# Two attention layers of a four-part kernel: batches staged in another order on TensorE, VectorE and ScalarE, with the group loops written out

## The chip, the core and the metric

The kernel runs on one core of a Trainium2 chip. The metric is the device time of one execution in microseconds (us). A core has five engines with queues of their own: PE (TensorE, matrix products; PEld is its weight loads), DVE (VectorE), ACT (ScalarE), POOL (GpSimd) and SP (SyncE, which here only issues transfers). Each queue is worked in the order of the program; engines wait for one another on semaphores, counters that one engine raises and another waits on. PE writes only to PSUM, eight banks of 512 float32 columns for 128 partitions.

## The reference, cut to what matters

```python
x = x + xattn0(layernorm(x), ctx)     # layer 0 attention
x = x + moe(layernorm(x))             # 32 experts, 4 per token
x = x + xattn1(layernorm(x), ctx)     # layer 1 attention
x = x + ternary_ffn(layernorm(x))

def xattn(hidden_q, kv_c, ...):       # 8 batches, 100 queries, 722 keys, 16 heads
    q_big  = einsum('bshk,hkq->bshq', (hidden_q @ Wq.T), w_kc_q)   # layer 0 also rotates it (rope)
    q_r    = einsum('bshq,hqr->bhsr', q_big, W_qr)
    k_r    = einsum('bld,hdr->bhlr', kv_rope, W_kr)
    scores = einsum('bhsr,bhlr->bhsl', q_r, k_r)
    attn   = softmax(scores, axis=-1)
    ctx_c  = einsum('bhsl,bld->bhsd', attn, kv_rope)
    ctx    = einsum('bhsd,hkd->bshk', ctx_c, w_kc_kv).reshape(b, s, H * K)
    return ctx @ Wo.T
```

Everything is float32 in the attention. The change touches only the two attention parts.

## The kernel before, in words

A layer's 16 heads are worked in four groups of four heads (`hg`, 0 to 3 in layer 0, 4 to 7 in layer 1). A group has four stages on PE.

**Head.** The projected queries `qc` of the group are made. In layer 0, `q_heads` (L643) makes a head's queries, `q_big` (L658) expands them, DVE and POOL rotate them, `q_r` (L670) and `q_c0` (L686) bring them to key space. In layer 1 there is no rotation, so two heads' weights are first folded into one matrix: `fold_m` (L700), `fold_mt` (L706), `fold_a` (L715), `fold_at` (L724), six pieces in all, each copied from PSUM by ACT (`fold`, through `copy`, L910) before the next can start. `q_r1` (L734) and `q_c1` (L748) then apply it. A group has two folds, u = 0 and 1, one for each pair of heads.

**Batches.** Eight batches `b` follow, staggered over ten steps `st`. The products of a batch are:

- `scores` (L757): six tiles of 128 keys by 400 columns (4 heads by 100 queries), which go in turn through PSUM banks 0, 1 and 2. Tile n waits until ACT has copied tile n - 3 out of its bank (semaphore `a_se`). ACT copies each tile into the SBUF buffer `Sb`, of which there are three (L991).
- DVE takes the largest value over the tiles, `mx` (L1056). PE transposes it (L842; semaphores `a_mx`, `a_mt`), DVE reduces it to `nmx`, with its sign changed (L1048), and PE spreads that over the partitions (L859; `a_nm`, `a_mb`).
- DVE adds it to the whole of `Sb` (L1052; `a_sb`), ACT takes the exponential in place (L1000; `a_ex`), DVE sums (L1065; `a_sum`).
- `softmax_sum` (L777) sums over partitions, DVE takes the reciprocal `rz` (L1062), `values` (L771) multiplies the exponentials with the keys for two halves `dc`, and DVE scales the result into `qc` (L1072; `a_cxe`).

In a step before, PE issues three tiles of batch st, the transposes of batch st - 1's maxima, the other three tiles, the spread, then `softmax_sum` and both halves of `values` of batch st - 2. DVE has the add of batch st - 1 ahead of the maxima of batch st. ACT has, in each step, the six copies of batch st, and behind them the exponential of batch st - 1.

**Tail.** In the last two steps there are no scores. PE puts a piece of the next group between: both halves of its first `q_heads` in layer 0, its first `fold_m` in layer 1.

**Output.** `ctxl` (L875) and the product with `Wo` (L885, L888) in fourteen pieces through banks 2 to 5, which DVE adds to `X` or `tail` (L1086; `a_add`). PE waits for all fourteen adds at the group's end (L891). SP then loads the next group's `wb` (L547) and, in layer 1, `wk` (L549), and behind them the weights of the group's second pair of heads (L535, L532).

PE, ACT, DVE, SP and POOL each run the groups in a hardware loop (`Fori`), with layer 0's first group written out ahead of it. In layer 1, POOL loads and ACT works pieces of the last layer's weights beside all that (`absolute`, L942): three per batch, with two buffers, each of which is loaded again only after ACT is done with it.

## Time and profile before

| | us |
|---|---|
| median of 3 runs | 3896.39 |
| lowest and highest | 3893.25, 3897.36 |
| the profiled execution | 3893.81 |
| its span, first to last instruction | 3892.1 |
| PE busy in it | 3594.0 (92%) |
| DVE busy | 1881.8 (48%) |
| ACT busy | 827.8 (21%) |
| layer 0's attention, about | 22 to 1333 |
| layer 1's attention, about | 2279 to 3302 |

The rows below have, for a timeline, the start and the time taken in us, the engine, the line, the operation, what it writes and reads, how many were merged into the row, and in brackets the idle time of the engine just before it with what ended it. `issue` is an idle time for which the profile shows no releaser. A float32 product here stands as two matmul records. PE's clock is shown by the granted clock of a stretch, of which 1.00 is full speed (2.4 GHz).

### The profile page before, as it was taken

The page shows a single profiled execution, that of the slowest core. Times are in us where ns is not written, and L with a number is a line of the kernel's source. Part 1 is how long each engine was busy: PE and PEld are TensorE (multiplying, and loading weights), DVE is VectorE, ACT ScalarE, POOL GpSimd, SP SyncE. Part 2 cuts the span into 40 slices and gives each one's busy share as a digit, 9 for nine tenths or more (in the row PEclk, how much of TensorE's full clock was granted, in tenths as well). Part 3 has the DMA queues.
Part 4 walks back from the last instruction along what each step waited for, and adds up shares of the span by engine and source line. Part 5 has one row for each costly group of instructions (what it writes and reads, how often), then busy time and mean ns, then how long its engine had stood idle before and what let it go on. Part 6 is the DMA issues. An engine that isn't in the chain of part 4 may idle for free.

```text
span 3892.1 us, 39006 instructions
## 1 busy us (share of the span) xinstructions
PE 3594.0 (92%) x14156; PEld 1763.2 (45%) x14157; DVE 1881.8 (48%) x1684; ACT 827.8 (21%) x1370; POOL 864.1 (22%) x778
## 2 busy tenths in 40 slices
PE   7899999999999869999999879999999998899999
PEld 4454455445445423333333335445455454554554
DVE  7784475466458441111111137538266285662561
ACT  1220131032022111111111125234143241220110
POOL 5500400310220022212222201000000000891780
PEclk9999999999999979999999989999999999999999
DMA  5621121122112186898779745245143250330320
GB/s 188 224 95 45 61 92 49 59 79 81 46 50 100 42 325 206 288 373 311 255 270 333 272 186 182 78 143 175 71 167 112 95 165 15 131 130 17 129 98 34
DMA packets 90366, 561.50 MB, mean 144 GB/s; under 512 B 10760, under 2 KB 12936, under 8 KB 76320
## 3 DMA queue, kind: packets, MB, share of 16 engines
q1 hardware_dynamic: 56080, 450.05, 30.3%
q0 software_dynamic: 30880, 93.75, 8.9%
q10 hardware_dynamic: 3312, 16.37, 1.2%
q8 instruction: 69, 1.13, 0.1%
q14 instruction: 25, 0.20, 0.0%
HBM read 522.39 MB, written 41.40 MB: 145 GB/s over the span
## 4 chain that ended last, share of the span: by engine, by line
PE 69%; DMA 10%; DVE 9%; issue 5%; POOL 5%; ACT 1%; SPq 1%; POOLq 0%; DVEq 0%; ACTq 0%
PE PS L771 12%; PE PS L757 11%; PE PS L1518 9%; PE PS L885 9%; PE PS L1895 4%; PE PS L1542 4%; DMA bias<-in_b 4%; POOL gtq L1814 4%; PE PS L643 3%; PE PS L658 3%; DVE mx L1056 2%; DMA stg<-in_F 2%; PE PS L875 2%; PE PS L734 2%; PE PS L1868 2%
## 5 line engine op out<-in xcount | busy, mean ns | idle before, releaser
L757 PE MATMUL PS<-qc,kvT 128*128 128x400 f32 x1536 | 544.9, 506 | 8.9 <-DMA kvT<-kvT_d 3.5
L1518 PE MATMUL PS<-W,hT 128*64 128x512 f32 x2208 | 514.4, 609 | 33.3 <-DMA bias<-in_b 32.8
L771 PE MATMUL PS<-Sb,kvN 128*128 128x400 f32 (+1 forms) x1536 | 529.6, 501 | 2.5 <-DVE qc L1072 2.5
L771 PEld LDWEIGHTS PS<-Sb,kvN 128*128 128x128 f32 (+1 forms) x1536 | 293.4, 191 | 231.7 <-issue 11.2
L1116 POOL TENSOR_TENSOR qrope<-rt,rt 128x400 f32<-128x400 f32 x192 | 209.9, 1114 | 827.8 <-DVE rt L1027 827.8
L757 PEld LDWEIGHTS PS<-qc,kvT 128*128 128x128 f32 x1536 | 290.0, 193 | 223.1 <-issue 22.6
L1607 DVE TENSOR_TENSOR gu<-PS,bias 128x512 f32<-128x512 f32 x69 | 47.7, 691 | 679.3 <-PE PS L1518 679.3
L1868 PE MATMUL PS<-xh,wq 128*128 128x400 f16 x2048 | 354.2, 335 | 18.6 <-DVE wq L1744 17.7
L1814 POOL TENSOR_SCALAR gtq<-stg,thr 128x1024 f16<-128x1024 f32 x96 | 311.7, 3259 | 114.6 <-DMA stg<-in_F 114.6
L885 PE MATMUL PS<-wb,ctxl 128*128 128x512 f32 x768 | 331.7, 593 | 4.7 <-ACT ctxl L910 4.7
L1056 DVE TENSOR_REDUCE mx<-Sb 128x400 f32<-128x2400 f32 x64 | 274.3, 4285 | 106.6 <-ACT Sb L991 106.6
L1518 PEld LDWEIGHTS PS<-W,hT 128*64 128x64 f32 x2208 | 155.4, 140 | 331.7 <-issue 300.4
L1868 PEld LDWEIGHTS PS<-xh,wq 128*128 128x128 f16 x2048 | 199.3, 98 | 173.4 <-issue 21.6
L1065 DVE TENSOR_REDUCE sums<-Sb 128x400 f32<-128x2400 f32 x64 | 265.6, 4149 | 0.0
L1027 DVE TENSOR_TENSOR rt<-PS,ropeq 128x800 f32<-128x800 f32 x192 | 180.8, 984 | 164.0 <-PE PS L658 163.9
L1542 PE MATMUL PS<-W,actT 128*64 128x512 f32 x1104 | 250.3, 596 | 2.5 <-ACT actT L1647 2.5
L991 ACT ACTIVATE Sb<-PS 128x400 f32<-128x400 f32 x320 | 159.0, 502 | 414.6 <-PE PS L757 414.6
L1052 DVE TENSOR_TENSOR Sb<-Sb,PS 128x2400 f32<-128x2400 f32 x64 | 169.9, 2654 | 158.3 <-PE PS L859 158.3
L885 PEld LDWEIGHTS PS<-wb,ctxl 128*128 128x128 f32 x768 | 145.3, 190 | 189.7 <-issue 179.9
L1086 DVE TENSOR_TENSOR X<-PS,X 128x512 f32<-128x512 f32 x96 | 66.4, 692 | 305.3 <-PE PS L885 305.3
L1744 DVE SCALAR_TENSOR_TENSOR wq<-stg,nthr,gtq 128x1024 f16<-128x1024 f32 x64 | 141.7, 2253 | 112.2 <-POOL gtq L1814 112.2
L1000 ACT ACTIVATE Sb<-Sb 128x2400 f32<-128x2400 f32 x64 | 141.1, 2205 | 237.4 <-DVE Sb L1052 237.4
(272 smaller groups left out, 3625.9 us busy)
## 6 DMA issues: line engine op xcount, KB each, us to landing
W<-in_W SPq DMA_DIRECT2D x34, 4096.0 KB
W<-in_W SPq DMA_DIRECT2D x34, 2048.0 KB
kvT<-kvT_d SPq DMA_DIRECT2D x64, 768.0 KB, 5.8
kvN<-kvN_d SPq DMA_DIRECT2D x64, 768.0 KB, 4.3
stg<-in_F SPq DMA_DIRECT2D x32, 1536.0 KB, 6.3
absin<-in_F POOLq DMA_DIRECT2D x48, 512.0 KB, 4.2
hn<-in_F POOLq DMA_DIRECT2D x48, 512.0 KB, 3.8
wb<-in_WB SPq DMA_DIRECT2D x8, 2560.0 KB, 9.4
```

The source lines that it names most:

```text
L757: mm = nc.tensor.matmul(PS[:, lc % 3, 0:GW], kvT[b % 2][:, dc, lc * P:(lc + 1) * P], qc[:, dc, b, :], start=dc == 0, stop=dc == CC - 1)
L771: mm = nc.tensor.matmul(PS[:, 6 + dc, 0:GW], kvN[b % 3][0:k, lc, dc * P:(dc + 1) * P], Sb[b % 3][0:k, lc, :], start=lc == 0, stop=lc == LC ...
L885: mm = nc.tensor.matmul(PS[:, 2 + n % 4, :], ctxl[:, a, m * P:(m + 1) * P], wb[:, w:w + 512], start=a == 0, stop=a == HA - 1)
L1027: ins = nc.vector.tensor_tensor(rt[k % 2][j][:, :, :].rearrange("p i (b s) -> p i b s", b=BH), src, tab, ALU.mult)
L1052: nc.vector.tensor_tensor(sb, sb, PS[:, 4, 0:GW].unsqueeze(1).to_broadcast([P, LC, GW]), ALU.add).then_inc(sem(f"{p}_sb"), 1)
L1056: nc.vector.tensor_reduce(mx[:, :], Sb[st % 3][:, :, :].rearrange("p c n -> p n c"), AX, ALU.max).then_inc(sem(f"{p}_mx"), 1)
L1065: nc.vector.tensor_reduce(sums[:, :], Sb[(st - 1) % 3][:, :, :].rearrange("p c n -> p n c"), AX, ALU.add).then_inc(sem(f"{p}_sum"), 1)
L1116: ins = nc.gpsimd.tensor_tensor(qrope[k % 4][:, i, :], rt[k % 2][0][:, i, :], rt[k % 2][1][:, 1 - i, :], ALU.add)
L1518: mm = nc.tensor.matmul(PS[g * BS:(g + 1) * BS, 2 + u % 2, :], hT2[k][:, c, half * BS:(half + 1) * BS], W2[:, q, o:o + N1], start=c == 0, ...
L1542: mm = nc.tensor.matmul(PS[h * BS:(h + 1) * BS, 4 + u % 2, :], actT[:, j, g * BS:(g + 1) * BS], W2[:, u % NQ_W, o:o + DH], start=c == 0, s ...
L1814: nc.gpsimd.tensor_scalar(gtq[q][:, w, :], stg[q][:, w, :], thr[:, w:w + 1], None, ALU.is_gt).then_inc(sem("f_gt"), 1)
L1868: mm = nc.tensor.matmul(PS[:, 4 * q + 2 * w + half, 0:HALF], wq[q][:, w, c, :], xh[part][:, c, half * HALF:(half + 1) * HALF], start=c == ...
```

## The change

- On PE, the six tiles of a batch's scores are issued together; behind them come the transposes of the previous batch's maxima, `softmax_sum` and the first half of `values` of the batch before that, the spread, and the second half of `values`.
- On DVE, the maxima of batch st are ahead of the add of batch st - 1, and the scaling into `qc` is ahead of the sums.
- On PE, the next group's pieces are spread over the last two batches. In layer 1 this is now the whole fold of its first pair, with PSUM banks 0 and 1, and ACT's six copies of it move with it; the SBUF tiles that it writes get places that the batches don't use.
- The wait for all of a group's adds moves from the group's end to the first products that write those banks; in layer 0 `q_big` starts with banks 4 and 5.
- PE's and ACT's group loops are written out; DVE, POOL and SP keep theirs.

The core of the diff:

```diff
+        def big_bank(k):
+            return 4 - 2 * (k % 2)
+
+        def fold_bank(u, n):
+            return ((1, 0, 1, 0, 1, 0), (1, 3, 4, 5, 2, 3))[u][n]
...
                 if k >= 2:
                     pe.wait_ge(sem(f"{p}_rt"), NQ * hg + k - 1)
+                elif hg > 0:
+                    pe.wait_ge(sem(f"{p}_add"), 2 * MT * hg - 2 * (1 - k))
...
+                for st in range(B):
+                    pe.wait_ge(sem(f"{p}_kt{st % 2}"), 16 * (4 * hg + st // 2 + 1))
+                    scores(hg, st, range(LC))
+                    if st == 0:
+                        continue
                     if st == 1 and ly == 1:
                         q_c1(hg, 6)
+                    largest(st - 1)
                     if st == 1 and ly == 1:
                         q_c1(hg, 7)
...
                     if st >= 2:
                         softmax_sum(hg, st - 2)
+                        values(hg, st - 2, 0)
+                    spread(st - 1)
+                    if st >= 2:
+                        values(hg, st - 2, 1)
+                largest(B - 1)
+                if more and ly == 0:
+                    q_heads(hg + 1, 0, 0, range(KC))
+                elif more:
+                    fold_m(hg + 1, 0)
+                values(hg, B - 2, 0)
+                if more and ly == 1:
+                    fold_mt(hg + 1, 0)
+                spread(B - 1)
+                values(hg, B - 2, 1)
+                softmax_sum(hg, B - 2)
+                if more and ly == 0:
+                    q_heads(hg + 1, 0, 1, range(KC))
+                elif more:
+                    fold_a(hg + 1, 0)
+                values(hg, B - 1, 0)
+                if ly == 0:
+                    softmax_sum(hg, B - 1)
+                elif more:
+                    fold_at(hg + 1, 0)
+                values(hg, B - 1, 1)
+                if ly == 1:
+                    softmax_sum(hg, B - 1)
...
-                pe.wait_ge(sem(f"{p}_add"), 2 * MT * (hg + 1))
-            with pe.Fori(g0 + (ly == 0), g0 + HG) as hg:
-                body(hg)
+            if ly == 1:
+                fold_all(g0, 0)
+            for hg in range(g0, g0 + HG):
+                body(hg, first=hg == 0)
```

On ACT, in a step `st`, nothing moves between the copies and the exponential, except that in layer 1 the copies of `q_c1`'s last two pairs go behind the six copies of step 1.

PE at the start of a group's batches, layer 0's first group, before. `kvT` is the key tile of `scores`, `mx` marks the transposes of the maxima, `nmx` the spread, `sums` the `softmax_sum`, `kvN` the `values`:

```order
L757 MATMUL PS<-qc_94,kvT_172416_95 128x400 x12
L757 MATMUL PS<-qc_94,kvT_178560_96 128x400 x6
L842 MATMUL PS<-cst_50,mx_65 100x128 x4
L757 MATMUL PS<-qc_94,kvT_178560_96 128x400 x6
L859 MATMUL PS<-cst_50,nmx_68 128x100 x4
L757 MATMUL PS<-qc_94,kvT_172416_95 128x400 x6
L842 MATMUL PS<-cst_50,mx_65 100x128 x4
L757 MATMUL PS<-qc_94,kvT_172416_95 128x400 x6
L859 MATMUL PS<-cst_50,nmx_68 128x100 x4
L777 MATMUL PS<-sums_66,cst_50 128x400
L771 MATMUL PS<-Sb_111616_71,kvN_184704_97 128x400 x12
```

The same place with the change:

```order
L767 MATMUL PS<-qc_93,kvT_172416_94 128x400 x12
L767 MATMUL PS<-qc_93,kvT_178560_95 128x400 x12
L844 MATMUL PS<-cst_50,mx_65 100x128 x4
L850 MATMUL PS<-cst_50,nmx_68 128x100 x4
L767 MATMUL PS<-qc_93,kvT_172416_94 128x400 x12
L844 MATMUL PS<-cst_50,mx_65 100x128 x4
L787 MATMUL PS<-sums_66,cst_50 128x400
L781 MATMUL PS<-Sb_111616_71,kvN_184704_96 128x400 x6
L850 MATMUL PS<-cst_50,nmx_68 128x100 x4
L781 MATMUL PS<-Sb_111616_71,kvN_184704_96 128x400 x6
```

The six tiles (twelve products) of a batch are no longer parted, and the second transposes of maxima have moved from the middle of batch 2's scores to behind them.

DVE at the same place, before:

```order
L1056 TENSOR_REDUCE mx_65<-Sb_111616_71 128x400
L1048 TENSOR_REDUCE nmx_68<-PS 100x4
L1052 TENSOR_TENSOR Sb_111616_71<-Sb_111616_71,PS 128x2400
L1056 TENSOR_REDUCE mx_65<-Sb_121216_72 128x400
L1065 TENSOR_REDUCE sums_66<-Sb_111616_71 128x400
```

DVE there with the change:

```order
L1086 TENSOR_REDUCE mx_65<-Sb_111616_71 128x400
L1082 TENSOR_REDUCE nmx_68<-PS 100x4
L1086 TENSOR_REDUCE mx_65<-Sb_121216_72 128x400
L1091 TENSOR_TENSOR Sb_111616_71<-Sb_111616_71,PS 128x2400
L1105 TENSOR_REDUCE sums_66<-Sb_111616_71 128x400
```

Batch 1's maxima have moved ahead of batch 0's add.

ACT there with the change; `Sb<-PS` are the copies, L1030 the exponential. The order is that of before, where the lines are L991 and L1000:

```order
L1017 ACTIVATE Sb_121216_72<-PS 128x400 x5
L1017 ACTIVATE Sb_121216_72<-PS,cst_50 128x400
L1030 ACT_TABLE_LOAD
L1030 ACTIVATE Sb_111616_71<-Sb_111616_71 128x2400
L1017 ACTIVATE Sb_130816_73<-PS 128x400 x5
```

Nothing has moved: batch 0's exponential still stands between the copies of batch 1 and those of batch 2.

## Rows read from the trace of the kernel before

**Rows 1.** The page, part 1: busy us, share of the span, instructions.
```profile
PE 3594.0 (92%) x14156; PEld 1763.2 (45%) x14157; DVE 1881.8 (48%) x1684; ACT 827.8 (21%) x1370; POOL 864.1 (22%) x778
```
**Rows 2.** Stretch 842.6:913.1: us; busy PE, PEld, DVE, ACT, POOL; PEclk, DMA, GB/s.
```profile
842.60:913.10 70.50, 70.50 (x234) 40.81 (x233) 59.82 (x25) 21.26 (x28) 0.00 (x0) 1.00 0.24 90
```
**Rows 3.** Timeline of PE, start of the batches, second group of layer 0.
```profile
482.53 12.35 PE L757 MATMUL PS<-qc,kvT 128*128 128x400 f32 x36 [0.66 <-ACT qc L910]
...
507.73 1.09 PE L842 MATMUL PS<-cst,mx 128*100 128x128 f32 x4 [2.85 <-DVE mx L1056]
...
524.30 2.18 PE L757 MATMUL PS<-qc,kvT 128*128 128x400 f32 x6
```
**Rows 4.** Timeline of DVE and ACT there.
```profile
491.52 4.23 DVE L1056 TENSOR_REDUCE mx<-Sb 128x400 f32<-128x2400 f32 x1 [17.02 <-ACT Sb L991]
496.48 0.69 DVE L1048 TENSOR_REDUCE nmx<-PS 100x4 f32<-100x512 f32 x1 [0.74 <-PE PS L842]
500.86 2.65 DVE L1052 TENSOR_TENSOR Sb<-Sb,PS 128x2400 f32<-128x2400 f32 x1 [3.69 <-PE PS L859]
...
503.55 2.20 ACT L1000 ACTIVATE Sb<-Sb 128x2400 f32<-128x2400 f32 x1 [2.44 <-DVE Sb L1052]
505.66 1.27 ACT L991 ACTIVATE Sb<-PS 128x400 f32<-128x400 f32 x3
```
**Rows 5.** Timeline of PE, the same start in the third group.
```profile
803.49 12.35 PE L757 MATMUL PS<-qc,kvT 128*128 128x400 f32 x36 [0.66 <-ACT qc L910]
...
842.59 2.85 PE L757 MATMUL PS<-qc,kvT 128*128 128x400 f32 x8
```
**Rows 6.** Timeline, the same start in layer 1's second group.
```profile
2583.96 12.35 PE L757 MATMUL PS<-qc,kvT 128*128 128x400 f32 x36 [0.79 <-DVE qc L1043]
...
2599.26 1.06 ACT L942 ACTIVATE hn<-hn 128x1024 f32<-128x1024 f32 x1 [3.76 <-DMA hn<-in_F]
...
2624.68 1.51 PE L757 MATMUL PS<-qc,kvT 128*128 128x400 f32 x4
```
**Rows 7.** Timeline of PE where layer 0's second, third and fourth groups start.
```profile
384.49 1.61 PE L658 MATMUL PS<-qhk,wc_h 128*128 128x400 f32 x4 [1.61 <-DVE hn L1086]
385.94 2.18 PE L643 MATMUL PS<-xnT,wq_h 128*128 128x400 f32 x6
...
702.67 3.03 PE L658 MATMUL PS<-qhk,wc_h 128*128 128x400 f32 x4 [5.80 <-issue]
705.49 3.58 PE L643 MATMUL PS<-xnT,wq_h 128*128 128x400 f32 x6
...
1020.42 3.03 PE L658 MATMUL PS<-qhk,wc_h 128*128 128x400 f32 x4 [5.24 <-issue]
```
**Rows 8.** DMA queues, 384 to 697 us: PE's instruction fetch (packets, MB, share).
```profile
q8 instruction: 8, 0.13, 0.2%
```
**Rows 9.** DMA queues, 2584 to 3089 us: there is no q8 row.
```profile
q14 instruction: 2, 0.02, 0.0%
```
**Rows 10.** Timeline of PE, layer 1, end of the first group, start of the second.
```profile
2466.56 0.93 PE L859 MATMUL PS<-cst,nmx 100*128 100x100 f32 x4 [4.40 <-DVE nmx L1048]
...
2539.57 1.92 PE L888 MATMUL PS<-wb,ctxl 128*32 128x512 f32 x16
2543.29 0.32 PE L706 MATMUL PS<-cst,mT_sb 128*128 128x128 f32 x1 [1.80 <-DVE hn L1086]
2543.98 3.04 PE L715 MATMUL PS<-wq_h,m_sb 128*64 128x512 f32 x8 [0.37 <-ACT m_sb L910]
...
2561.08 1.53 PE L700 MATMUL PS<-wc_h 128*64 128x128 f32 x24
```
**Rows 11.** DMA, 2530 to 2575 us: KB each, us to landing; 2544 to 2557, all packets.
```profile
wb<-in_WB SPq DMA_DIRECT2D x1, 2560.0 KB, 9.0
...
DMA packets 850, 4.99 MB, mean 384 GB/s; under 512 B 92, under 2 KB 92, under 8 KB 727
```
**Rows 12.** Timeline of PE, layer 0's last group, the spread of batch 7.
```profile
1254.70 0.93 PE L859 MATMUL PS<-cst,nmx 100*128 100x100 f32 x4 [5.83 <-DVE nmx L1048]
```

More of the change, by code:

```diff
@@ L229, in build @@
         wk = pl1.put("wk", [P, HA // 2, DC])
+        mT_sb = pl1.put("mT_sb", [P, K])
+        m_sb = pl1.put("m_sb", [P, 2 * R])
         pa.at = max(pa_sb.at, pl0.at, pl1.at)
@@ L235, in build @@
         wb = pa.put("wb", [P, WB_N])
+        aT_sb = pa.put("aT_sb", [P, D])
         ropek = pprep.put("ropek", [P, 2, LC, DC])
@@ L777, in softmax_sum, with fold_all @@
                 nc.tensor.matmul(PS[:, 5, 0:GW], ones, sums[:, :], start=True, stop=True).then_inc(sem(f"{p}_z"), 1)
-            def next_group(hg, n):
-                if ly == 0:
-                    q_heads(hg, 0, n, range(KC))
-                elif n == 0:
-                    fold_m(hg, 0)
+            def fold_all(hg, u):
+                fold_m(hg, u)
+                fold_mt(hg, u)
+                fold_a(hg, u)
+                fold_at(hg, u)
             def body(hg, first=False):
@@ L814, in body @@
                 else:
-                    fold_mt(hg, 0)
-                    fold_a(hg, 0)
-                    fold_at(hg, 0)
                     q_r1(hg, 0)
@@ L849, in body @@
                         pe.wait_ge(sem(f"{p}_qce"), 16 * hg + 16)
-                    if st >= B:
-                        if first:
-                            next_group(hg + 1, st - B)
-                        else:
-                            with pe.If(hg < g0 + HG - 1):
-                                next_group(hg + 1, st - B)
-                    if 1 <= st <= B:
-                        pe.wait_ge(sem(f"{p}_nm"), B * hg + st)
-                        for a in range(HA):
-                            mm = nc.tensor.transpose(PS[:, 4, a * S:(a + 1) * S], nmx[0:S, a:a + 1].to_broadcast([S, P]), ident[0:S, 0:S])
-                        mm.then_inc(sem(f"{p}_mb"), 1)
                     if st >= 2:
                         softmax_sum(hg, st - 2)
-                        for dc in range(CC):
-                            values(hg, st - 2, dc)
+                        values(hg, st - 2, 0)
[25 more added lines that the diff above has]
+                    softmax_sum(hg, B - 1)
                 pe.wait_ge(sem(f"{p}_wb"), 16 * (hg + 1))
@@ L967, in body @@
                 else:
-                    for n in range(6):
-                        fold(hg, 0, n)
                     c_qr1(hg, 0)
@@ L983, in body @@
                         c_qc1(hg, n, 0)
+                more = hg < g0 + HG - 1
                 for st in range(B + 1):
@@ L992, in body @@
                                                  bias=bias).then_inc(sem(f"{p}_se"), 1)
-                            if st == 1 and ly == 1 and lc % 3 == 2:
-                                for j in range(2):
-                                    c_qc1(hg, 6 + lc // 3, j)
+                            if st == 1 and ly == 1 and lc == LC - 1:
+                                for n in range(6, 8):
+                                    for j in range(2):
+                                        c_qc1(hg, n, j)
                             if ly == 1 and lc in (1, 4):
                                 absolute(hg, 3 * st + lc // 3)
+                    if st == B and ly == 1 and more:
+                        for n in range(2):
+                            fold(hg + 1, 0, n)
                     if st >= 1:
@@ L1005, in body @@
                         eng.dma_start(acc_t[bass.ds(hg * ZROWS, ZROWS), :], A["zero"].to_broadcast([ZROWS, D])).then_inc(sem("m_fill"), 16)
+                if ly == 1 and more:
+                    for n in range(2, 6):
+                        fold(hg + 1, 0, n)
                 for n in range(2 * HA):
@@ L1008, in body @@
                     copy(ctxl[:, a, half * HALF:(half + 1) * HALF], PS[:, 3 + n % 2, 0:HALF], "lt", 8 * hg + n + 1, "lte")
-            if ly == 0:
-                body(0, first=True)
-            with eng.Fori(g0 + (ly == 0), g0 + HG) as hg:
-                body(hg)
+            if ly == 1:
+                for n in range(6):
+                    fold(g0, 0, n)
+            for hg in range(g0, g0 + HG):
+                body(hg, first=hg == 0)
         def att_vector(dve, ly):
```

76 lines of the change are left out of this document (36 added, 40 removed).

## The prediction, made before the changed kernel was run

> **What bounds the kernel now.** I read the page's busy times first: PE is busy for 92% of the span, 298 us are left over [rows 1], so an attention change can only win by closing PE's gaps. Then I read the windows over the middle of a group. Over four batches, 70.5 us or 17.6 us each, PE is busy for all of 70.5 us at full clock, DVE for 59.8 [rows 2]. There nothing waits, and the order of the products can't matter unless it makes a wait. So the question is what the change does at three places: the start of the batches, their end, and the passage to the next group. There the timeline of PE shows its gaps, and the timelines of DVE and ACT show what ends them.
>
> The start, from the first score tile to that of batch 3, holds 34.6 us of work on PE: three scores of 8.06, one `values` of 8.06, one `softmax_sum` of 0.7, and transposes. It takes 39.1 us in the undisturbed case [rows 5], 41.8 in the second group, where the clock was low after an idle 2.85 [rows 3], and 40.7 in layer 1 with 1.75 more work [rows 6]. The other five, read the same way, are 42.2 and 40.5 in layer 0, and 41.7, 40.5, 40.5 in layer 1.
>
> **The steady batches.** The same products, adds and reductions are issued. In the new order, counted from the start of batch st's scores, PE does: scores to 8.1, transposes of maxima to 8.5, `softmax_sum` and half of `values` to 13.2, spread to 13.6, other half to 17.6. DVE: nmx 8.7 to 9.4, maxima 4.23 long to 13.7, add 2.65 long to 16.4, reciprocal, scaling, sums to 24.2, that is 6.6 in the next batch; PE wants them at 8.5. ACT's exponential is over at 18.6, and the first copy of the next batch is due at 19.3. Every wait has slack: 0 us, with 17.6 per batch as before.
>
> **The start of the batches: a new wait.** This is the term against the change. DVE now does batch 1's maxima ahead of batch 0's add, ACT has the exponential of batch 0 ahead of the copies of batch 2, and at this point PE has no `values` to fill in. Layer 0, from the first score tile at 0, durations from [rows 4], offsets as there (maxima start 9.0 after the scores, nmx 0.67 after its transposes, the add 0.54 after the spread):
> - PE: scores 0 and 1 to 16.1, transposes to 16.6. nmx is 16.8 to 17.5, so PE idles 1.0 until the spread at 17.6. Scores 2 start at 18.0.
> - DVE: maxima of batch 1 from 17.5 to 21.7, add of batch 0 to 24.3. Before, that add began with the spread [rows 4].
> - ACT: exponential of batch 0 from 24.4 to 26.6. Only then comes the copy of batch 2's first tile, over at 27.1.
> - PE: three tiles fit into banks 0 to 2 by 22.0, the fourth waits for that copy: 5.2 us idle. Scores 2 end at 31.2, `softmax_sum`, `values`, two transposes end at 40.8.
>
> 40.8 against 39.1 is 1.7 us more. And the low clock comes on top: after idle times of 5.80 the next products took 3.03 and 3.58 us for 1.61 and 2.18, a loss of 2.8 [rows 7]; after 2.89 there was none [rows 5]. An idle 5.2 lies near the first, I take 2.2, bounds 0 and 2.8. So 43.0 per group, four make 172, and the first group keeps another 1.7 us of low clock from its wait for the keys. 173.7 against 163.6 before: **+10**, bounds +1 and +12.
>
> Layer 1 is worse, because ACT's pieces of `absolute` stand in its queue. The fourth waits for its data until 15.3 after the start, and is over at 16.5 [rows 6]; copies behind it are late. Before, PE had `q_c1` and transposes to do there. Now the sixth tile of batch 1 waits for the copy of its third: 2.1 idle. Then ACT copies tiles, a fifth piece (1.25), the last tile at 19.5, and `q_c1`'s pairs; PE idles 0.9 for them; spread 21.3, scores 2 from 21.7. Maxima 20.5 to 24.8, add to 27.4, exponential to 29.7, one more piece of `absolute` to 30.7, first copy over at 31.2; the fourth tile has waited since 25.7, 5.5 us. Scores 2 end at 35.2, batch 3 starts at 45.0. With 2.2 of low clock 47.2, four times 188.8, against 163.4: **+25**, bounds +8 (the data comes in time, no low clock) and +29.
>
> **Batches' end.** Layer 0 before loses 0.45 and some transposes' order; counted through in the new order, with the scaling ahead of the sums, PE never waits: 46.6 from the last scores to `ctxl` against 47.3, -0.7 for each of three passages, **-2**. Layer 1 before idles 4.40 at the spread of batch 7 [rows 10], with low clock behind it, 44.2 in all. Now `fold_mt`, `fold_a`, `fold_at`, 3.4 us, stand in its place; I count idles of 0.6, 0.35 and 1.9 and 43.6 us: -0.6 each. In the last group of a layer there is nothing to put between: idles of 2.1, 0.8 and 3.7 where one of 5.83 stood [rows 12]: 0, bounds -1 and +1 for both.
>
> **The passage, layer 0.** The first passage waits 1.61 for the adds [rows 7]; `q_big` in banks 4 and 5 needs twelve of the fourteen, which are there when PE is done: -1.6. The second and third are jumps back in the loop, and idle 5.80 and 5.24 with no releaser, then run 2.8 and 2.7 at low clock [rows 7]. Such a group has 8 fetches of instructions [rows 8]; the first group, written out, has its fetches and no such idle. Written out, these go: -8.6 and -7.9. What is late next is DVE, whose loop stays: its rotation could start up to some us later, but `q_big` needs it only from its third product on, 5.4 us in; 0, at most +1.5 each. Sum **-18**, bounds -18 and -15.
>
> The Trainium skill, page "Runtime: NRT & Kernel Launch", section "Instruction fetch mechanics", says that a taken branch whose target is outside a window of two pages forces a fetch, and that kernels therefore rather unroll. By it layer 1's three jumps would stall too, and writing them out would give some 12 us more. The trace doesn't bear that out: those three idle 1.80 at most, no more than their adds need [rows 10], and in 505 us there is not one fetch on q8 [rows 9].
>
> **The passage, layer 1.** Before, from the end of L888 at 2541.5, PE waits 1.80, folds with low clock, and reaches the second `fold_m` at 2561.08, 19.6 later [rows 10]. The folds are gone from here, so `q_r1` (10.9) starts at once and `fold_m` could come 12 us in. But it reads weights that SP asks for only behind `wb` and `wk`, after the last add: `wb` lands 9.0 after 2542.93, and 1.97 MB behind it at the 384 GB/s of this stretch need 5.1 [rows 11]: 2557.0, 15.5 after PE's end. So 4.1 are won, and an idle 3.2 in front of `fold_m` may bring low clock, 1.8: 2.3, bounds 1 and 7.9. With the batches' end: -2.9 each, three make **-9**, bounds -5 and -25.
>
> The Trainium skill, "DMA: Bandwidth & Descriptors", section "Where 436 GB/s comes from", has 436 GB/s as the ceiling; by it the 5.1 would be 4.5, and the sum 2 us less.
>
> **Sum.** +10 +25 -2 -18 -9 = +6 us. The profiled execution was 3893.8, its span 3892.1 and 1.7 around it; it lay 2.6 under the median of 3896.4. 3893.8 + 6 = 3900; against the median 3902. I predict 3901.
>
> **Rivals.**
> 1. *The start costs little.* The low clock doesn't come after the new idle, and `absolute`'s data is there. For it: one of four groups in layer 0 and three of four in layer 1 had none after 2.9 idle; against: after the attention's idles of 3.5, 4.4, 5.2 and 5.8 the clock was low each time. Then the starts cost +1 and +8, the passages stay: +9 -29 = -20, 3876. With only half of that, 3890, it would just count as no change. 18%.
> 2. *The start costs more* (the slower side, beyond my own forecast). ACT's queue in layer 1 is a chain: if a transfer for `absolute` lands later, the first copy of batch 2 is later by the same, and PE's idle grows one for one. It decides from about 1 us more per group, or when low clock comes twice in one start, after 2.1 and after 5.5: 2.8 more. +3 in each of eight groups is +24: 3920 or so with the rest. 20%.
> 3. *Steady batches get a wait*, because DVE's chain runs 1.9 us ahead of PE's need, no more. Each 0.2 us per batch would be 64 x 0.2 = 13: 3914. Against: 59.8 of 70.5 busy [rows 2]. 7%.
> 4. *Writing out does not remove the idle* at layer 0's jumps, because it is something else than the jump: +16.5, 3917. For it: `issue` names no releaser. Against: the first passage, without a jump back, has none. 7%.
>
> My forecast has 48%. Its own range is 3893 to 3909. What a measurement can tell from no change is 0.2%, 7.8 us, so from 3888.6 to 3904.2. The forecast's part below 3904 is same, about 30 of 48, the rest slower; rivals 2 to 4 are slower; rival 1 is faster but for its nearest end. Faster 0.17, same 0.38, slower 0.45. Range for 8 in 10: 3884 to 3918, leaving out rival 1's far end and the worst of 2.
>
> **What would show it.** Steady batches of 17.6 us, PE full. At each start, an idle of about 5 us in front of the fourth tile of batch 2, ended by ACT's copy, with ACT's exponential of batch 0 right ahead of it, and the granted clock low behind it; 43 us from first tile to batch 3 in layer 0, 47 in layer 1. No idle from `issue` at layer 0's passages, some 9 q8 fetches in each group of layer 1. In layer 1's passages, `fold_m` waiting some 3 us for `wc_h`. I am wrong if that idle in batch 2 is under 3 us, or batches take another time than 17.6.

## The result, and the profile after

| | before | changed |
|---|---|---|
| median of 8 runs, us | 3890.61 | 3905.47 |
| lowest and highest | 3884.23, 3897.36 | 3903.10, 3918.24 |
| ratio to before, 95% interval | | 1.0048, 1.0037 to 1.0059 |
| the profiled execution, its span | 3893.81, 3892.1 | 3903.10, 3901.4 |

The changed kernel is slower by 0.5%, 14 to 23 us by the interval. The forecast of 3901 lay 4.5 below the time, but part of that is luck: its difference of +6 stands against a measured +15 by the medians (+19 by the ratio), and it was added to a base of 3896, the median of three runs, which is 5.8 above the median of the eight. The stretches below are read from PE's timelines. "Start" is from the first score tile to batch 3's first, "end" from there to the first product with `Wo`, "passage" from the last of those to the next group's first score tile.

| sum of the stretches, us | before | changed | difference | forecast |
|---|---|---|---|---|
| four starts, layer 0 | 163.5 | 171.8 | +8.2 | +10 |
| four starts, layer 1 | 163.4 | 187.5 | +24.1 | +25 |
| ends of three groups, layer 0 | 387.8 | 385.7 | -2.0 | -2 |
| three passages, layer 0 | 310.8 | 295.7 | -15.1 | -18 |
| ends of three groups, layer 1 | 378.4 | 382.3 | +3.8 | -2 |
| three passages, layer 1 | 127.4 | 121.0 | -6.4 | -7 |
| two last groups' ends | 252.4 | 255.5 | +3.1 | 0 |
| ahead of the first scores | 168.2 | 169.6 | +1.5 | 0 |
| between the two attentions | 1000.7 | 993.1 | -7.6 | 0 |

The rest is -0.3. The attention's stretches alone, from the first start on, make +16. The last row is code that the change doesn't touch: it took from 993 to 1001 us in the fourteen profiles of this case. Such a difference belongs to an execution, and I leave it out of the reasons.

The page of the changed kernel, part 1; PE is busy for 8.1 us more than before [rows 1], with the same 14156 instructions:

```profile
PE 3602.1 (92%) x14156; PEld 1768.0 (45%) x14157; DVE 1892.4 (49%) x1684; ACT 825.1 (21%) x1367; POOL 864.0 (22%) x778
```

The start of the third group's batches in the changed kernel, PE (columns as before: start, us, engine, line, operation, merged count, idle time ahead and what ended it), which answers to [rows 5]:

```profile
795.78 16.44 PE L767 MATMUL PS<-qc,kvT 128*128 128x400 f32 x48 [0.55 <-ACT qc L937]
812.05 0.60 PE L844 MATMUL PS<-cst,mx 128*100 128x128 f32 x4
813.53 0.53 PE L850 MATMUL PS<-cst,nmx 100*128 100x100 f32 x4 [0.88 <-DVE nmx L1082]
813.89 4.22 PE L767 MATMUL PS<-qc,kvT 128*128 128x400 f32 x12
822.74 5.99 PE L767 MATMUL PS<-qc,kvT 128*128 128x400 f32 x12 [4.62 <-ACT Sb L1017]
...
838.11 1.17 PE L767 MATMUL PS<-qc,kvT 128*128 128x400 f32 x3
```

DVE there, and ACT, answering to [rows 4]:

```profile
813.30 4.19 DVE L1086 TENSOR_REDUCE mx<-Sb 128x400 f32<-128x2400 f32 x1
817.42 2.64 DVE L1091 TENSOR_TENSOR Sb<-Sb,PS 128x2400 f32<-128x2400 f32 x1
```
```profile
820.09 2.20 ACT L1030 ACTIVATE Sb<-Sb 128x2400 f32<-128x2400 f32 x1 [7.24 <-DVE Sb L1091]
822.20 1.27 ACT L1017 ACTIVATE Sb<-PS 128x400 f32<-128x400 f32 x3
```

Read it backwards from PE's 4.62 of idle at 822.74. It ends when ACT's copy frees a bank. The copy stood behind the exponential (820.09), that waited 7.24 for DVE's add (817.42), and the add stood behind batch 1's maxima (813.30), though the spread it needs was over at 814. The three tiles had lain in PSUM since 818. Each link is a queue worked in its order.

The granted clock behind that idle, and in the steady batches, answering to [rows 2] (stretch, us; busy PE, PEld, DVE, ACT, POOL; PEclk, DMA, GB/s):

```profile
822.70:828.80 6.10, 6.07 (x15) 3.34 (x16) 3.83 (x1) 1.82 (x5) 0.00 (x0) 0.72 0.00 0
842.00:913.00 71.00, 71.00 (x235) 41.04 (x234) 61.21 (x25) 21.52 (x29) 0.00 (x0) 1.00 0.29 106
```

A row x12 has twelve records, which are six products. With the granted clock at 1.00, its 2.4 GHz level, such a row takes 4.2 to 4.3 us. Behind that idle it took 5.99; 0.72 is the mean of a stretch that was partly at the 1.2 GHz level. The steady batches are as before, PE full.

PE in the changed kernel at other places: layer 1's start in its second group [rows 6], layer 0's second and third passage [rows 7], layer 1's second fold [rows 10], `values` of batch 7 in layer 1's first group, the same in layer 0's last group [rows 12], and the last `q_r`, `q_c0` and scores at the head of layer 0's second group:

```profile
2590.03 1.61 PE L767 MATMUL PS<-qc,kvT 128*128 128x400 f32 x4 [1.31 <-ACT Sb L1017]
2604.22 6.35 PE L767 MATMUL PS<-qc,kvT 128*128 128x400 f32 x12 [5.14 <-ACT Sb L1017]
...
696.67 1.61 PE L666 MATMUL PS<-qhk,wc_h 128*128 128x400 f32 x4
1009.93 1.61 PE L666 MATMUL PS<-qhk,wc_h 128*128 128x400 f32 x4
...
2549.48 2.03 PE L708 MATMUL PS<-wc_h 128*64 128x128 f32 x24 [3.30 <-DMA wc_h<-in_WC]
...
2467.82 5.96 PE L781 MATMUL PS<-Sb,kvN 128*128 128x400 f32 x12 [2.09 <-DVE qc L1101]
...
1257.36 7.33 PE L781 MATMUL PS<-Sb,kvN 128*128 128x400 f32 x12 [3.96 <-DVE qc L1101]
...
474.17 2.10 PE L678 MATMUL PS<-qrope,wc_h 128*64 128x400 f32 x8 [2.57 <-POOL qrope L1149]
476.92 3.04 PE L694 MATMUL PS<-qr,wc_h 64*128 64x400 f32 x8 [0.64 <-issue]
480.51 18.75 PE L767 MATMUL PS<-qc,kvT 128*128 128x400 f32 x48 [0.56 <-ACT qc L937]
```

The queue of PE's instructions in the changed kernel, in a group of layer 0 and in two of layer 1 [rows 8, 9]; the prediction had some 9 for one group of layer 1, where these are 13 for two:

```profile
q8 instruction: 8, 0.13, 0.2%
q8 instruction: 13, 0.21, 0.2%
```

### The profile page after: what moved, and what is told of

Same layout as the page of the kernel before. It is cut to its first block, busy times and chain, and to the rows that moved or that the text cites. A ratio compares the mean times of both kernels' runs of the same rounds, so it can differ in the third digit from the quotient of the medians.

```text
span 3901.4 us, 37786 instructions
## 1 busy us (share of the span) xinstructions
PE 3602.1 (92%) x14156; PEld 1768.0 (45%) x14157; DVE 1892.4 (49%) x1684; ACT 825.1 (21%) x1367; POOL 864.0 (22%) x778
## 4 chain that ended last, share of the span: by engine, by line
PE 67%; DMA 14%; DVE 8%; POOL 5%; issue 4%; ACT 1%; SPq 1%; POOLq 0%; DVEq 0%; ACTq 0%
PE PS L781 13%; PE PS L767 12%; PE PS L914 9%; PE PS L1551 7%; DMA acc_d<-ysb,sidxc 5%; PE PS L1928 4%; POOL gtq L1847 4%; PE PS L649 4%; PE PS L1575 4%; PE PS L666 3%; DMA bias<-in_b 3%; DMA stg<-in_F 2%; PE PS L904 2%; DMA hs<-h_d,idxc 1%; PE PS L678 1%
## 5 line engine op out<-in xcount | busy, mean ns | idle before, releaser
L781 PE MATMUL PS<-Sb,kvN 128*128 128x400 f32 (+1 forms) x1536 | 550.4, 509 | 20.0 <-DVE qc L1101 20.0
L767 PEld LDWEIGHTS PS<-qc,kvT 128*128 128x128 f32 x1536 | 298.7, 196 | 292.8 <-ACT Sb L1017 51.4
L1847 POOL TENSOR_SCALAR gtq<-stg,thr 128x1024 f16<-128x1024 f32 x96 | 310.8, 3250 | 115.5 <-DMA stg<-in_F 115.3
L1030 ACT ACTIVATE Sb<-Sb 128x2400 f32<-128x2400 f32 x64 | 141.0, 2203 | 467.3 <-DVE Sb L1091 467.3
L1098 DVE RECIPROCAL rz<-PS 128x400 f32<-128x400 f32 x64 | 169.8, 2653 | 56.8 <-PE PS L787 56.8
```

The lines of the kernel that those rows point to most:

```text
L767: mm = nc.tensor.matmul(PS[:, lc % 3, 0:GW], kvT[b % 2][:, dc, lc * P:(lc + 1) * P], qc[:, dc, b, :], start=dc == 0, stop=dc == CC - 1)
L781: mm = nc.tensor.matmul(PS[:, 6 + dc, 0:GW], kvN[b % 3][0:k, lc, dc * P:(dc + 1) * P], Sb[b % 3][0:k, lc, :], start=lc == 0, stop=lc == LC ...
L1098: nc.vector.reciprocal(rz[:, :], PS[:, 5, 0:GW]).then_inc(sem(f"{p}_rz"), 1)
L1847: nc.gpsimd.tensor_scalar(gtq[q][:, w, :], stg[q][:, w, :], thr[:, w:w + 1], None, ALU.is_gt).then_inc(sem("f_gt"), 1)
```

## The experiments

Each was timed beside the kernel before; ratios are to before, with the 95% interval. The kernel before had medians of 3887.9 to 3890.6 beside the different experiments, so two kernels are compared by their medians and, where that says something else, by their ratios. Sums of starts, ends and passages are from one profile each.

| kernel | median, us | ratio (interval) | starts layer 0, 1 |
|---|---|---|---|
| e1, add first in step 1 | 3865.67 | 0.9936 (0.9922 to 0.9951) | 161.2, 170.3 |
| e2, exponential later | 3892.34 | 1.0005 (0.9995 to 1.0016) | 171.0, 178.2 |
| e3, before, PE written out | 3879.19 | 0.9968 (0.9955 to 0.9981) | 164.7, 164.5 |
| e4, fold at head | 3917.04 | 1.0070 (1.0055 to 1.0086) | 178.3, 188.1 |
| e5, absolute later | 3902.40 | 1.0028 (1.0016 to 1.0041) | 176.9, 180.5 |
| e6, sum ahead of second half | 3886.02 | 0.9992 (0.9982 to 1.0003) | 176.8, 186.7 |
| e7, e1 with e5 and e6 | 3849.75 | 0.9893 (0.9878 to 0.9908) | 160.9, 171.2 |
| e8, before, maxima first | 3923.61 | 1.0086 (1.0072 to 1.0100) | 175.1, 181.6 |
| e9, e7 with the start filled | 3831.62 | 0.9858 (0.9843 to 0.9874) | 148.9, 149.7 |
| e10, e7 with early weights | 3840.27 | 0.9881 (0.9865 to 0.9897) | 155.8, 174.1 |
| e11, e9 and e10 | 3818.11 | 0.9822 (0.9808 to 0.9837) | 148.7, 149.7 |
| e12, e11 with the fold at the head | 3850.86 | 0.9905 (0.9890 to 0.9920) | 147.7, 149.7 |

### e1 and e8: which reordering makes the wait

e1 is the changed kernel with DVE's old order in one step (`a_mb` is what the add waits for, `a_se` what the maxima wait for):

```diff
+                    if st == 1:
+                        dve.wait_ge(sem(f"{p}_mb"), B * hg + st)
...
                     if st < B:
                         dve.wait_ge(sem(f"{p}_se"), LC * B * hg + LC * (st + 1))
...
-                    if 1 <= st <= B:
+                    if 2 <= st <= B:
                         dve.wait_ge(sem(f"{p}_mb"), B * hg + st)
```

> The changed kernel, but DVE adds to batch 0 ahead of batch 1's maxima (step 1 only, all eight groups). My theory (the lost time is a wait that DVE's order makes at the start of the batches, since ACT's exponential of batch 0 stands ahead of the copies of batch 2): in layer 0 the add ends at 20.8 after the first tile, the exponential at 23, PE's fourth tile of batch 2 no longer waits, and the start takes 38.5 to 39.5 us instead of 42 to 44.5; in layer 1 the exponential and a piece of absolute end at 27, the fourth tile waits some 2 us instead of 5.1, and the start takes 42 to 44 instead of 47. Together -30 us, bounds -20 and -34: 3875 where the changed kernel has 3905. Rival A (ACT's queue is the cause, whatever DVE does first): under 1 us per group, 3900. Rival B (the six tiles standing together cost time on PE itself): nothing changes, 3905.

3865.67, 40 us under the changed kernel by the medians, beyond the bound of 34. In the profiles, of which one is the slowest run of e1 and the other the fastest of the changed kernel, the starts give 27.8; what the other 12 are, one profile of each doesn't show. PE at the fourth group's start in e1:

```profile
1120.59 4.22 PE L767 MATMUL PS<-qc,kvT 128*128 128x400 f32 x12
1126.13 4.30 PE L767 MATMUL PS<-qc,kvT 128*128 128x400 f32 x12 [1.32 <-ACT Sb L1017]
...
1131.85 0.94 PE L787 MATMUL PS<-sums,cst 128*128 128x400 f32 x2 [0.99 <-DVE sums L1110]
```

The idle 4.6 is now 1.32, and the clock stays up. This start took 38.5 us, as worked out; the other three of layer 0 took 40.3 to 41.4, since their first 48 records took 18.2 to 19.3 us for 16.4. In layer 1 the same idle is 2.35 for 5.14, near the 2 expected.

e8 is the counterpart, the kernel before with maxima first (in all steps) and nothing else of the change:

```diff
-                        dve.wait_ge(sem(f"{p}_mb"), B * hg + st)
...
                     if st < B:
                         dve.wait_ge(sem(f"{p}_se"), LC * B * hg + LC * (st + 1))
...
+                    if 1 <= st <= B:
+                        dve.wait_ge(sem(f"{p}_mb"), B * hg + st)
...
```

> The kernel before, with one thing of the change alone: DVE takes the maxima of batch st ahead of the add of batch st-1, in all steps. PE and ACT keep their old order and loops. My theory (the maxima first are what hurts, not the six tiles together): the steady batches stay at 17.6 us; at each start PE's idle 2.85 in front of the transposes of batch 1's maxima goes, but the fourth tile of batch 2 waits some 4.9 us for ACT's copy behind the exponential: 1.8 us more per group, with the low clock up to 4, and more in layer 1: +10 to +30, 3911. Rival (the six tiles together make the loss, as PE then has nothing between them): no more than +4, 3892.

3923.61, +33.7, a little over the range and the slowest kernel of all. PE in e8, the same start as [rows 5]:

```profile
828.08 0.64 PE L842 MATMUL PS<-cst,mx 128*100 128x128 f32 x4 [0.52 <-DVE mx L1052]
833.27 6.25 PE L757 MATMUL PS<-qc,kvT 128*128 128x400 f32 x12 [4.54 <-ACT Sb L991]
```

The same wait for the same copy, while the six tiles are still parted by the transposes. Its starts are 29.8 us longer than before's, the changed kernel's 32.3. So DVE's order makes a loss of this size by itself. The six tiles together show no cost in layer 0: with DVE's old order (e1) its starts are 2.3 us under before's. In layer 1 they seem to cost some 6 us for four groups, low clock included (the changed kernel is 5.9 over e8, e1 6.9 over before): there the sixth tile waits for a copy that stands behind late `absolute` data, a wait in which PE once had `q_c1` and transposes to do.

### e2: ACT's place for the exponential

```diff
+                            if st == 2 and lc == 2:
+                                exponential(0)
```

Before, this exponential was at the end of step 1, ahead of step 2's copies.

> The changed kernel, but ACT takes batch 0's exponential behind the first three copies of batch 2 (DVE's order as changed). My theory: the fourth tile of batch 2 is free to go, but DVE's sums of batch 0 then come 4.2 us behind the exponential, and softmax_sum of batch 0 waits for them some 4 us; the start takes 40 to 42.5 us in layer 0 (42 to 44.5 now) and 44 to 46 in layer 1 (47 now): -8 to -20 together, 3891. So the chain maxima, add, exponential, sums of DVE and ACT is what is late, and the idle time moves to its next user. Rival A (only ACT's queue is at fault): the starts return to the 41 us of before, -32, 3873. Rival B (the tiles together cost on PE): 3905.

3892.34, -13, within the range; starts of 41.7 to 44.4 in layer 0, partly above the 40 to 42.5 expected, and of 44.4 to 44.8 in layer 1. By the profiles the starts of layer 0 gain 0.8 us in all and those of layer 1 9.3; another 6.3 are layer 0's passages, which this edit doesn't touch. PE in e2, third group:

```profile
823.19 1.70 PE L787 MATMUL PS<-sums,cst 128*128 128x400 f32 x2 [4.00 <-DVE sums L1111]
```

The idle has moved to the next user, DVE's sums, 4.0 for 4.6 us. So the wait for a bank was only the first point at which PE met the late chain, and ACT's queue alone (rival A) isn't the cause.

### e3: PE's loops alone

```diff
-            with pe.Fori(g0 + (ly == 0), g0 + HG) as hg:
+            for hg in range(g0 + (ly == 0), g0 + HG):
```

The branch in the loop that tells the last group from the others (`pe.If`) goes with it.

> The kernel before, with nothing changed but PE's group loops, which are written out. My theory: the idle 5.80 and 5.24 us at layer 0's second and third passage and the low clock behind them (2.8 and 2.7) go, DVE's last adds may keep up to 1.6 of each: -13 to -16.5 us, 3876 where before has 3891. Layer 1's three passages stay at 42.45 us each, though their jumps go as well. Rival A (the idle is not the jump's): nothing, 3891. Rival B (a taken branch always forces a fetch, so layer 1's jumps cost too, hidden in its waits): layer 1's passages get shorter as well, by 1 to 4 us each: 3868.

3879.19, -11 (-12 by the ratio, 7 to 17 us by its interval), just short of the range. In its profile layer 0's passages are 99.23, 99.22 and 97.85 against 99.66, 106.63 and 104.53: -14.5, as expected. Layer 1's are 2.4 less together. Starts and ends took 6.6 us more, at waits that the kernel before has as well, with more low clock behind them. PE in e3, layer 0's second passage, and layer 1's first:

```profile
699.40 1.61 PE L658 MATMUL PS<-qhk,wc_h 128*128 128x400 f32 x4 [1.31 <-DVE hn L1083]
...
2532.21 0.33 PE L706 MATMUL PS<-cst,mT_sb 128*128 128x128 f32 x1 [1.31 <-DVE hn L1083]
```

The idle is now DVE's add and 1.31 everywhere, 4.5 and 3.9 less in layer 0 [rows 7], 0.5 less in layer 1 [rows 10]. I had expected layer 1's jumps back to cost nothing. Going by the idle time, one cost 0.5 us at most, and layer 0's first passage, which is no jump back, lost 0.3 as well [rows 7]. By the Trainium skill, "Runtime: NRT & Kernel Launch", section "Instruction fetch mechanics", a jump to outside the window stalls on a fetch; layer 0's did, and layer 1's loop shows no fetch at all [rows 9]. Written out, layer 1 has 13 fetches in two groups, without an idle time of `issue`: the section calls crossing a block mostly hidden, and the trace agrees.

### e5 and e6: the two smaller waits

e5 (layer 1; pieces 3 and 4 of `absolute` go behind step 1's copies) and e6 (one line moved in PE's end):

```diff
+                                for k in range(3, 5):
+                                    absolute(hg, k)
-                            if ly == 1 and lc in (1, 4):
+                            if ly == 1 and lc in (1, 4) and st != 1:
```
```diff
                 spread(B - 1)
-                values(hg, B - 2, 1)
                 softmax_sum(hg, B - 2)
+                values(hg, B - 2, 1)
```

> The changed kernel, but ACT's two pieces of absolute that stand between the copies of batch 1 (layer 1) come behind its six copies and the copies of q_c1. My theory: PE's idle times of 1.3 us in front of batch 1's last tile and 0.9 in front of the spread go, everything behind comes 1.5 to 2 us earlier, and the 5.1 us in front of batch 2's fourth tile stay; a start in layer 1 takes 43 to 45.5 us instead of 47: -6 to -14, 3895. Layer 0 as it was. Rival (the late data of absolute only shifts the wait, the first copy of batch 2 comes just as late): 3905.

3902.40: -3 by the medians, -8 by the ratios to before, with intervals that overlap. That is at the low edge of -6 to -14 or short of it. Layer 1's starts are 44.7 to 45.8, -7.0 together, as expected. In front of batch 2's fourth tile PE still idles, 5.22 in e5's second group of layer 1. The range was right for the stretch; only -3 to -8 shows in the time.

> The changed kernel, but behind the last spread PE takes the softmax_sum of batch 6 ahead of the second half of its values. My theory: the idle 2.09 us in front of batch 7's values in layer 1's first three groups, and 3.96 in each layer's last group, are waits for the chain softmax_sum, reciprocal, scaling of batch 6, which then starts 4 us sooner. 2.1 to 3.9 us (with the low clock behind it) for each of three groups, 2.4 to 5.5 in each last group, nothing in layer 0's first three, where a piece of the next group covers it: -11 to -22, 3889. Rival (DVE's reciprocal has to wait for its add of batch 7 anyway, and scaling for both halves of values): 0 to -4, 3903.

3886.02, -19.5. PE in e6, layer 1's first group:

```profile
2457.61 0.86 PE L787 MATMUL PS<-sums,cst 128*128 128x400 f32 x2
2458.30 4.20 PE L781 MATMUL PS<-Sb,kvN 128*128 128x400 f32 x12
2462.43 1.94 PE L725 MATMUL PS<-wq_h,m_sb 128*64 128x512 f32 x8
2464.30 4.30 PE L781 MATMUL PS<-Sb,kvN 128*128 128x400 f32 x12
```

No idle is left in front of the last row, and it takes 4.30 where it took 5.96. Each of layer 1's first three ends is 3.8 us shorter, 2.1 of idle and 1.7 of clock; layer 0's last group is 5.2 shorter, layer 1's 3.7.

### e7: do they add up

> The changed kernel with three edits at once: DVE adds to batch 0 ahead of batch 1's maxima, ACT's two pieces of absolute come behind the copies of batch 1, and softmax_sum of batch 6 stands ahead of the second half of its values. If the waits are separate ones in PE's path, as my theory has it, they add up: from the measured -40 for the first and -6 to -14 and -11 to -22 for the others: -57 to -76, 3839, 1.3% under the kernel before. Rival (the low clock comes back elsewhere when one idle time goes, as it is set by something else): no more than -45, 3860.

3849.75, -56 by the medians, -60 by the ratios; the three singly came to -62 and -73. So most of it adds up, and the rival's -45 is ruled out. By the medians it is just short of the range, by the ratios within it.

### e4 and e12: what the spread fold is worth

```diff
                 else:
+                    if hg > g0:
+                        fold_all(hg, 0)
                     q_r1(hg, 0)
...
-                elif more:
-                    fold_m(hg + 1, 0)
...
```

`fold_mt`, `fold_a` and `fold_at` and ACT's six copies go with it.

> The changed kernel, but in layer 1 the whole fold of a group's first pair of heads stands at the group's head again, one piece behind the other, for three groups; nothing of it between the last batches. My theory: spread over the last batches the fold was free (last batches with it take 45.5 us, the last group's without it 45.6), and at the head it is serial: the batches' end stays at 45.5, the passage goes from 40.3 to about 44 us: +11 us, bounds +6 and +14, 3916. Rival A (between the batches the fold costs what it saves at the head, as the end grew by 1.3 us against the kernel before): 3905, with the batches' end at 44.2. Rival B (the passage is limited by the weights that arrive late for the second fold alone, so it stays at 40 to 42): +0 to +5.

3917.04, +12, within the range, and yet the theory isn't shown by it. Its passages took 41.35 each, not 44, 3.1 more for the three; the ends of those groups stayed as they were, as expected. The rest of its time lies in layer 0's starts (+6.5), between the attentions (+5.3) and in the last group, which e4 doesn't touch. By the profile rival B holds, and the interval overlaps with the changed kernel's. PE in e4:

```profile
2549.63 11.01 PE L744 MATMUL PS<-xnT,a_sb 128*128 128x400 f32 x32 [0.69 <-ACT a_sb L931]
2560.57 0.94 PE L758 MATMUL PS<-qr,wk 64*128 64x400 f32 x4
2561.44 1.53 PE L708 MATMUL PS<-wc_h 128*64 128x128 f32 x24
```

`q_r1` begins 6.6 us behind the last product with `Wo`, but the second `fold_m` doesn't wait: the weights had those 6.6 us to land. Spread, the fold had bought time that PE then spent waiting 3.3 us for them.

e12 asked again, where those weights no longer come late (e11).

> The same as the kernel with both, but in layer 1 the fold of the first pair of heads stands serially at the group's head again, for three groups (and SP's early request so waits for it there). It asks what spreading the fold is worth once the late weights no longer cover it. My theory: the fold at the head is 6.7 us of PE time and waits for ACT's copies per group, 4.8 of them work that is done in either case, and in the batches' end its place is taken by waits again: +2 to +6 per group, +6 to +18 together, 3824. Rival (spreading is worth nothing, the added time at the head is given back at the end): 0 to +3, 3813.

3850.86, +33 against e11: the range was +6 to +18, so this was a miss. The passages are 10.4 us longer each (136.4 for three against 105.1), the ends of those groups 1.7 longer together. PE in e12, layer 1's first passage:

```profile
2503.22 11.01 PE L753 MATMUL PS<-xnT,a_sb 128*128 128x400 f32 x32 [0.69 <-ACT a_sb L943]
2516.23 1.11 PE L767 MATMUL PS<-qr,wk 64*128 64x400 f32 x4 [2.00 <-DMA wk<-in_WK]
2517.27 2.83 PE L717 MATMUL PS<-wc_h 128*64 128x128 f32 x24
```

6.6 are the fold. 2.0 are a wait for `wk`, which SP now asks for only behind a wait for that fold, and 1.5 the low clock behind it. So here some 4 us per group come from my edit of SP's queue and not from the fold. The other error was in the price: it counted on part of the fold's 6.6 us coming back at the ends, and the ends gave nothing back.

### e9, e10 and e11: better than both

e9, start of the batches: `exponential(0)` behind two copies of batch 2, no piece of `absolute` ahead of it or of those copies, and on PE

```diff
+                    if st == 2:
+                        values(hg, 0, 0)
+                        softmax_sum(hg, 0)
```

> The three edits together (3850), and the start of the batches changed further: ACT takes batch 0's exponential behind two copies of batch 2 instead of ahead of all, PE issues the first half of batch 0's values ahead of softmax_sum, and in layer 1 no piece of absolute stands ahead of that exponential or those copies. My theory (a start is limited by the chain nmx, add, exponential, sums of batch 0, and PE stands still only because it asks for its results in the wrong order): PE's idle of 1.3 (layer 0) and 2.4 to 3.4 us (layer 1) in front of batch 2's fourth tile goes, and that at softmax_sum too; 36 to 38 us per start in layer 0 (40.2 now), 38 to 40 in layer 1 (42.8 now): -20 to -35, 3822. Rival (DVE is full there, so the wait comes back one batch later at softmax_sum of batch 1): no more than -8, 3842.

3831.62: -18 by the medians and -14 by the ratios, short of the range; the starts did as expected, 35.7 (twice; 38.5 and 39.0 with low clock) and 37.2 to 38.0, -33.5 together (by its profile, the fastest of its runs, against e7's, the slowest). Some of the gain was lost again behind them: batch 3 to the end of layer 1's batches grew from 493.5 to 499.4, so the rival had a part. PE in e11, which has the same start, layer 0's third group:

```profile
797.12 8.25 PE L776 MATMUL PS<-qc,kvT 128*128 128x400 f32 x24
805.21 0.60 PE L853 MATMUL PS<-cst,mx 128*100 128x128 f32 x4
805.64 4.20 PE L790 MATMUL PS<-Sb,kvN 128*128 128x400 f32 x12
```

e10, SP asks for the second pair's weights early:

```diff
+                    if ly == 1:
+                        second_pair(hg + 1)
                     sp.wait_ge(sem(f"{p}_add"), (hg + 1) * 2 * MT)
                     group(hg + 1)
```

`second_pair` waits for the fourth piece of the first pair's fold, and then loads `wc_h` and `wq_h`.

> The three edits together (3850), and SP asks for the weights of a layer 1 group's second pair of heads as soon as the spread fold of the first pair has read its own, ahead of wb and wk. My theory (the passage in layer 1 is held by weights that queue behind wb): the idle 3.3 us in front of the second fold_m goes, and with it 1 us of low clock where it came; wk, which now lands 9 us after the last add, is there before q_r1 ends at 11: the passage takes 36 to 37 us instead of 38.2 to 41.4 (39.8): -8 to -13 for three, 3839. Rival (the granted clock of this stretch falls for another reason and DVE's and ACT's copies set the pace of q_c1): -3 at most, 3847.

3840.27, -9.5 by the medians, within the range, but -5 by the ratios, short of it and with intervals that overlap. In its profile the passages took 34.81, 34.88 and 34.73, even 1.2 us under the range, where e7 has 119.3 for the three. The wait is shown to be gone; what that is worth in the time is known only roughly. PE in e11 there:

```profile
2507.02 0.94 PE L767 MATMUL PS<-qr,wk 64*128 64x400 f32 x4 [0.37 <-DMA wk<-in_WK]
2507.89 1.53 PE L717 MATMUL PS<-wc_h 128*64 128x128 f32 x24
```

> Both of the last two: the start of the batches filled and the weights of layer 1's second pair asked for early. If they are independent, as my theory has it: -28 to -48 against the three edits together, 3812, 2.0% under the kernel before and 2.4% under the changed one. Rival: one of them takes the other's gain through the clock: 3830.

3818.11, -32 against e7 by the medians, -28 by the ratios, where e9 and e10 singly sum to -28 and -18. Neither takes the other's gain. It is 1.8% under the kernel before (ratio 0.9822) and, over before's ratio, 2.2% under the changed one.

## Why the prediction was right, and where it was not

**The start.** Shown, link by link: +32 in the profile for +35 predicted, the idle in front of batch 2's fourth tile 4.62 for 5.2 in layer 0 and 5.14 for 5.5 in layer 1, with low clock behind each of these seven. The clock cost 1.4 to 1.7 us in layer 0 and 2.1 to 3.0 in layer 1, where the sum had 2.2 for both. The first group of layer 0 idles only 2.78 there, because its keys came late and cost 1.60 before, and its clock stayed up: 40.6 us, where the sum had 44.7. In the second and fourth group the first 48 records took 18.75 and 18.88 us for 16.4, low clock that came into the start from a wait in the head; no term had these 4.8. So layer 0's 171.8 for 173.7 is in part luck, two misses that cancel. e8 makes the wait alone, e1 takes most of it away, e2 moves it. The prediction named the new order on DVE and the exponential in ACT's queue together; e8 and e1 show that the first decides. Of layer 1's +24, some 6 are the six tiles' wait for `absolute`, which stood in the sum as well.

**Steady batches.** 17.6 us, PE full, as predicted.

**Layer 0's passages.** The jumps' idle is gone, as e3 shows too. -15.1 for -18: more low clock behind a wait that had no term. PE waits 2.57 for POOL's rotation in front of the last `q_r`, in the change as before. The kernel before, second group:

```profile
476.64 2.94 PE L670 MATMUL PS<-qrope,wc_h 128*64 128x400 f32 x8 [2.58 <-POOL qrope L1116]
480.26 1.61 PE L686 MATMUL PS<-qr,wc_h 64*128 64x400 f32 x8 [0.68 <-ACT qr L910]
```

It had low clock in this `q_r` in two of three groups (2.94 us for 1.56) and none in `q_c0`. The changed kernel had it in all three: `q_r` took 1.97 to 2.72 and `q_c0` 3.04, where e2 has 1.56 and 1.61 after the same 2.57. The change of order is no reason for that, since e2 has nearly all of it too.

**Layer 1's passages.** -6.4 for -6.9, with the predicted wait for `wc_h` (3.30 for 3.2). It fits the 384 GB/s of [rows 11]; the prediction's other rate, 436 GB/s, would have made it 2.6. e10 shows it was SP's order.

**The ends: the step that failed.** "I count idles of 0.6, 0.35 and 1.9 and 43.6 us: -0.6 each", and for the last groups "idles of 2.1, 0.8 and 3.7 ... : 0". The idles came out nearly so: 0.57, 0.24 and 2.09, and 2.03, 0.35 and 3.96. But I set no low clock behind them. It came after 2.09 three times of three (5.96 for 4.27 us) and after 3.96 in both last groups (in layer 0, 7.33). So the ends made +3.8 for -1.8 and +3.1 for 0, 8.7 of the 10 us by which the attentions came out above the sum. e6 gives back what idle and clock had cost: 2.1 and 1.7 in each.

**The chances.** The prediction's own parts don't add up: rivals 2 to 4 (34%) and the forecast's slower part (18) make 52% for slower, not 45, and some 31% for same, not 38. Rival 2's +24 on the forecast is 3925, not 3920.

**Rivals.** The start costing little didn't happen, nor did a wait in the steady batches, nor an idle that stays at the jumps. The start costing more didn't either; the extra loss lay at the ends, by the same means as that rival's second low clock.

**What stays open.** When the clock falls after an idle of 1.5 to 2.6 us. The profile of a kernel is one execution; those of e3, e5 and e9 lie 4 to 7 us from their medians, and the executions of one kernel spread by 5 to 20 us. Nothing I ran tells how much of the 15 us between the medians is low clock of this kind, and how much are the waits of the new order. Behind the wait for POOL alone the changed kernel's profile has some 8 us more of it than before's. That the changed kernel is slower is shown, and that its starts lose through DVE's order; the split of the 15 us is not. The later wait for the adds was not tried by itself either; by the profiles it is worth the idle 1.31 that e3 keeps in each passage and the changed kernel doesn't have.

## What to carry to other kernels

Before moving an operation ahead of another on one engine, look at the fill of the pipeline and not at its steady state: with all slack there in the middle, the first rounds can still have a chain that runs through two other queues back to a PSUM bank. Two experiments settle such a case: the suspected edit alone in the old kernel, and undone alone in the new one. Price an idle time of PE with the clock behind it: here idles of 2.1 to 5.2 us had 1.4 to 3.1 us of low clock behind them.

## What the runs showed of the hardware

Rows of twelve records with 128x400 results (4.2 to 4.3 us at full clock), in all fourteen profiles, by the idle time shown just ahead of them: under 1.5 us, 48 of 48 took the full-clock time; from 3 us up, 52 of 52 took 5.7 to 7.3; from 1.5 to 2.5, 29 of 55 took 5.9 to 6.0. The one row between (2.78) took 4.30. Of the 42 waits of 2.57 us for POOL in layer 0's passages, 24 had low clock behind them: the `q_r` took 1.63 to 2.94 us for 1.56, in 17 of them `q_c0` took 3.04 for 1.61 as well, and in 15 it reached into the scores. So between 1.5 and 2.6 us the same instruction at the same place falls either way. In e1, `values` of batch 7 in layer 1's first and third group:

```profile
2452.40 4.27 PE L781 MATMUL PS<-Sb,kvN 128*128 128x400 f32 x12 [2.09 <-DVE qc L1106]
...
2959.27 5.96 PE L781 MATMUL PS<-Sb,kvN 128*128 128x400 f32 x12 [2.10 <-DVE qc L1106]
```

That is 1.7 us for one time that the clock falls; behind the wait for POOL it was up to 4.3. The profiles have on average six idle times of 1.5 to 2.5 us from a layer's first scores to its last product with `Wo` (87 in fourteen; none in e3, 14 in e12), and three waits for POOL each. That could make a good part of the spread between executions of one kernel, but it is not shown: e3, with none of the first kind, spread by 11 us, e12 by 10.
